# New start addresses for the stationary sides of TensorE's in, state and up projections

## What is computed

```python
xz = layernorm(x) @ w_in                          # w_in 256 x 1024
xp, z = split(xz)                                 # 512 and 512
xc = silu(causal_conv(xp, 4 taps) + conv_b)
h[t] = 0.9 * h[t-1] + 0.1 * (xc[t] @ w_B)         # 16 states
x = x + ((h @ w_C) * silu(z)) @ w_out             # w_out 512 x 256
# per sequence, the two best of 8 experts by its first token:
x = x + mean over 2 experts of (gelu(layernorm(x) @ W1[e] + b1[e]) @ W2[e] + b2[e])
```

## Time and profile before

| | |
|---|---|
| median of 3 runs | 509.88 us (509.74 to 510.04) |
| the profiled execution | 509.51 us |
| its span, first to last instruction | 507.6 us |
| PE busy | 502.6 us, 99% |
| PE weight loads | 447.5 us, 88% |
| VectorE busy | 450.1 us, 89% |
| ScalarE busy | 401.2 us, 79% |
| GpSimd busy | 343.0 us, 68% |
| chain that ended last | PE 97%, VectorE 2%, DMA 1% |

### The profile page before, as it was taken

How to read it: one execution, slowest core, us unless ns; L and a number is a source line. 1 busy time by engine, 2 the same in 40 slices (tenths; PEclk the granted TensorE clock), 3 DMA queues, 4 the chain that set the end, 5 groups by cost and what they waited for, 6 DMA issues and landing times.

```text
span 507.6 us, 9831 instructions
## 1 busy us (share of the span) xinstructions
PE 502.6 (99%) x3026; PEld 447.5 (88%) x3026; DVE 450.1 (89%) x898; ACT 401.2 (79%) x694; POOL 343.0 (68%) x386
## 2 busy tenths in 40 slices
PE   8999999999999999999999999999999999999997
PEld 8888799899998989989899998989989899898997
DVE  6999999989998899979999899997999889896773
ACT  4986958878969788697887969879797887969454
POOL 4956587659693696928969197772977549673391
PEclk9999999999999999999999999999999999999999
DMA  8940105335251542606234170432604333130102
GB/s 260 297 174 1 42 1 167 124 126 167 71 188 35 165 124 83 206 14 196 79 124 165 42 224 24 165 124 86 203 36 149 104 125 125 50 116 0 43 2 83
DMA packets 53378, 57.27 MB, mean 113 GB/s; under 512 B 8682, under 2 KB 49642, under 8 KB 53226
## 3 DMA queue, kind: packets, MB, share of 16 engines
q1 hardware_dynamic: 51498, 56.67, 34.3%
q10 hardware_dynamic: 1856, 0.31, 0.3%
HBM read 35.46 MB, written 21.50 MB: 112 GB/s over the span
## 4 chain that ended last, share of the span: by engine, by line
PE 97%; DVE 2%; DMA 1%; issue 0%; DVEq 0%
PE blk L1267 16%; PE blk L1268 16%; PE blk L1272 16%; PE tok L1384 12%; PE tok L1386 12%; PE tok L1385 12%; PE turn L1425 3%; PE turn L1428 3%; PE blk L1447 3%; PE turn L1219 1%; PE tok L1267 1%; PE tok L1268 1%; PE tok L1272 1%; DMA x_mid<-in_L_attn_x 1%; DVE stats_t L893 0%; DVE normed L910 0%
## 5 line engine op out<-in xcount | busy, mean ns | idle before, releaser
L968 DVE SCALAR_TENSOR_TENSOR conv<-blk,tap_w,conv 128x512 f32<-128x512 f32 x192 | 130.0, 741 | 9.1 <-ACT conv L659 8.4
L470 POOL TENSOR_TENSOR y_lo<-gate,y_hi 128x512 fp32r<-128x512 f32 x57 | 72.1, 1297 | 36.1 <-ACT y_hi L588 36.1
L1267 PE MATMUL blk<-xn_hi,w_in_hi 128*128 128x512 f32 x228 | 89.4, 392 | 0.0
L1268 PE MATMUL blk<-xn_hi,w_in_lo 128*128 128x512 f32 x228 | 89.0, 391 | 0.0
L435 POOL TENSOR_TENSOR xc_lo<-conv,xc_hi 128x512 fp32r<-128x512 f32 x59 | 70.5, 1211 | 9.1 <-ACT xc_hi L588 9.0
L1384 PE MATMUL tok<-w_out_hi,y_hi 128*128 128x256 f32 x256 | 72.1, 282 | 0.0
L1386 PE MATMUL tok<-w_out_hi,y_lo 128*128 128x256 f32 x256 | 71.9, 281 | 0.0
L1385 PE MATMUL tok<-w_out_lo,y_hi 128*128 128x256 f32 x256 | 71.9, 281 | 0.0
L1272 PE MATMUL blk<-xn_lo,w_in_hi 128*128 128x512 f32 x228 | 70.3, 389 | 0.0
L1384 PE MATMUL tok<-w_hi,hid_hi 128*128 128x256 f32 x248 | 70.0, 282 | 0.0
L659 ACT ACTIVATE conv<-blk,tap_b,tap_w 128x512 f32<-128x512 f32 x64 | 49.0, 777 | 26.2 <-PE blk L1272 23.7
(11 more groups left out here) (187 smaller groups left out, 1316.9 us busy)
## 6 DMA issues: line engine op xcount, KB each, us to landing
spill<-normed SPq DMA_DIRECT2D x25, 512.0 KB, 2.8
normed<-spill SPq DMA_DIRECT2D x100, 128.0 KB, 2.8
out<-x_mid SPq DMA_DIRECT2D x30, 256.0 KB, 2.7
x_mid<-in_L_attn_x SPq DMA_DIRECT2D x29, 256.0 KB, 2.7
x_in<-in_L_attn_x SPq DMA_DIRECT2D x14, 512.0 KB, 4.4
w_all<-in_L_ffn_W SPq DMA_DIRECT2D x2, 2048.0 KB, 11.5
b_all<-in_L_ffn_b SPq DMA_DIRECT2D x1, 1024.0 KB, 13.3
gate<-in_L_attn_w_in SPq DMA_DIRECT2D x2, 256.0 KB, 4.4
```

Source lines behind the costliest of these rows:

```text
L470: nc.gpsimd.tensor_tensor(y_lo[:, j, :], gate_of(o, j), y_hi[:, j, :].bitcast(F32), ALU.subtract).then_inc(y_lo_set, 1)
L968: nc.vector.scalar_tensor_tensor(cols, blk[j][:], tap_w[:, j, t:t + 1], cols, ALU.mult, ALU.add).then_inc(tap_added, 1)
L1267: mm(dst, whi(k), his(k), start=(k == 0), stop=False)
L1268: mm(dst, wlo(k), his(k), start=False, stop=False)
```

## The change

Two declarations become longer by 16 numbers (64 bytes) in each row, and the buffer of 64 bytes moves ahead of them. The views that the rest of the program uses have the same shapes as before.

```diff
+STEP = 16
...
-        w_in_hi, w_in_lo = sb("w_in_hi", [P, KD, 2 * DI], F32R), sb("w_in_lo", [P, KD, 2 * DI], F32R)
-        w1_hi, w1_lo = sb("w1_hi", [P, TOP_K, KD * D], F32R), sb("w1_lo", [P, TOP_K, KD * D], F32R)
+        behind_columns = sb("behind_columns", [P, STEP])
+        w_in_hi, w_in_lo = [sb(f"w_in_{part}", [P, KD, 2 * DI + STEP], F32R)[:, :, 0:2 * DI] for part in ("hi", "lo")]
+        w1_hi, w1_lo = [sb(f"w1_{part}", [P, TOP_K, KD * D + STEP], F32R)[:, :, 0:KD * D] for part in ("hi", "lo")]
         b_mix = sb("b_mix", [P, JD, P], F32R)
         c_mix = sb("c_mix", [P, DI], F32R)
-        behind_columns = sb("behind_columns", [P, 16])
```

## The result

The changed kernel takes 512.32 us in the median of 5 runs (512.11 to 512.55), the kernel before 509.92 us beside it (509.74 to 510.19): a ratio of 1.0047, with a 95% interval of 1.0036 to 1.0058. It is 2.4 us slower, where 2.1 us faster was forecast. The profiled execution took 512.32 us too.

A forecast was written before the change was run, and what follows sets the result against it. PE's start-to-start matmul distances were taken as the bound. 509.51 - 1.5 (new offsets) - 0.6 (run openings) = 507.4 us profiled; the median stands 0.37 us above, so 507.8 us, range 503.5 to 515.0.

The forecast's parts named there:

- What bounds the kernel: Whole program: PE's matmul row is busy 99% of the span, so start-to-start distances make the time; copies cost nothing.
- wrong at the root: Sign of failure: PE has new waits, or 512-column matmuls keep 226.6 ns while the time moves.
- The price of a new offset: 512-column matmuls whose loads get new offsets: gain of 1.2 ns each, 1270 x 1.2 ns = 1.5 us.
- The bound from below: 512-column matmuls: 226.6 ns is twice 113.3 ns, the best 256-column rhythm, so the gain may be 0.
- The bound for a loss: 512-column matmuls out of step with their loads cost 231.7 ns, 5.1 ns more.
- The openings: First matmuls of 512-column runs behind 256-column ones, some 42 in the program: half of 1.2 us saved, 0.6 us.
- The rival that the rhythm never settles: xp, z and up of every step: differing loads disturb each matmul, up to 5.1 ns each, 516.5 us; chance 0.35.
- The rival of the token matmuls' better rhythm: 256-column matmuls go from 117.7 to 113.3 ns, 6.4 us less, 503.5 us; chance 0.10.
- Offsets don't matter: All matmuls: new addresses change nothing since the read ports are independent, 509.9 us; chance 0.15.
- What would show it: Up projection with `state_in`: 7.21 us or less means gain, 7.25 no effect, 7.30 and above rhythm lost.
- the slower case: 512-column matmuls lose their steady rhythm, up to 516.5 us, chance 0.35; touched loads of 192 instead of 188 ns would support it.

The follow-up runs named there:

- the small matmuls: Kernel before plus one matmul of 8 or 64 columns (second kernel: 32 or 128) ahead of looped 256-column runs: 508.53 and 508.85 us.

## Why the prediction was wrong

- *What bounds the kernel.* Right: PE's distances alone, with no cost at the copies. The one new wait of PE, 0.5 us in the opening, would have been a sign of being wrong at the root by the prediction's own words, but the first projection starts no later with it.
- *The price of a new offset.* This is the step that failed: "I take half of the gain, 1.2 ns per matmul". The sign was wrong. The price came from 256 columns, 2.3 ns cheaper at 64 than at 0, with the reason that a load is as long beside a long matmul as beside a short one. The runs show that the relation turns round with the width: at 512 columns 64 costs 6.6 ns more than 0 (516.1 us with all at 64). That loads are equally long at both widths was true (188 ns) and said nothing of what a matmul costs. The bound from below had it nearly right: 226.6 is twice 113.3, and no offset tried gave less than 226.7, so there was nothing to gain. The bound for a loss, 5.1 ns from an opening, was close to what the new offsets cost, though for another reason, since there it is an opening and here a lasting price: w_in, w1, b_mix and c_mix lost 5.48 us over 1332 matmuls, 4.1 ns each.
- *The openings.* The 0.6 us saved didn't come. The first six matmuls of z take 1394 ns now and took 1388 before, and behind them the run doesn't come back to 226.7: it repeats a pattern of six distances (229, 237, 229, 234, 228, 229, ...) at 231 ns.
- *The rival that the rhythm never settles* happened, 4.1 ns of its 5.1. It would give 509.51 + 5.5 = 515.0 us alone. (Its upper end for the profiled execution is 509.51 + 6.8 = 516.3 us, not 516.5.) Its reason was only half right: it blamed loads that differ from one another, but loads all alike at 64 are worse (516.1), and the variation helps as far as it brings in cheap offsets. Only for w1's second expert did it cost something of its own.
- *The rival of the token matmuls' better rhythm* happened as well, for the 36 of `down` and the 12 behind `state_out` in the looped steps, 2.45 us. The prediction gave it a chance of 0.10 and no part in the sum; without it the change would have cost some 4.9 us. The argument against it, that the usual run starts behind a steady run of 512 columns, holds for the kernel before but doesn't tell the cases apart: behind b_mix at a steady 233.3 ns (all at 64) `down` stays at 117.8, behind b_mix at a nearly steady 232.8 in the changed kernel it goes at 113.4. And that a run's rhythm is set as it starts is contradicted by the prediction's own, where it changes within the run.
- *Offsets don't matter.* Refuted: two kernels with the same instructions differ by 6.2 us (516.1 against 509.9). The Trainium skill (TensorE: Matmul & The Clock Gate, What happens when you issue a matmul) says that the two read ports are independent. What the prediction drew from it, that no offset can count, the measurement decides against; the page itself speaks of read bandwidth and not of start addresses.
- *What would show it.* 7.45 us for the up projection with `state_in` was read rightly as the rhythm lost. "192 would speak for the slower case" was wrong: with all at 64 z's loads last 188 ns at 233.3 ns a matmul, as they did at 227.8. In the changed kernel 36 of w1's 288 loads between 108 and 469 us last 192 ns, where none did before.

What stays open: why offset 0 is the cheapest for 512 columns and not for 256, and why two offsets 256 bytes apart cost nearly the same. That what stands ahead of a run can decide between 113.3 and 117.7 ns is shown by the small matmuls; which entries lead to which rhythm isn't. The moving sides stood at one place in every kernel, so it isn't shown whether the stationary side's own start counts or its distance from the moving side's.

## What to carry to other kernels

Where back-to-back matmuls bound a kernel, measure the distance from start to start for each kind of matmul, and vary the start address of the stationary side: a price for an offset holds for the width at which it was measured, and may turn round at another. Before a steady rhythm is given up, see whether it is the best that the kernel's rows show for that shape. And look at what stands ahead of a long run: a few slightly dearer matmuls, or one tiny one, can put the next 36 or 47 into a better rhythm, and a change can win there what it loses at its own place.

## What the runs showed of the hardware

- With the moving side at one place, a matmul's cost depends on the stationary side's start: 226.7 to 234.0 ns at 512 columns, 113.3 to 120.2 at 256. At 512 columns two starts 256 bytes apart cost the same within 1 ns.
- At 256 columns and offset 64 there are two steady rhythms at the same addresses, 113.3 and 117.7 ns. Behind one matmul of 8 to 128 columns the looped runs were always in the better one; a load 35 ns late ahead of a run, or distances of 121 to 125 ns in the middle of one, went with a change to the better one too.
- A matmul of 8 columns costs 27 ns itself and 85 ns more in the next one, and saves some 4 ns in each of the 47 behind.
- At 256 columns and offsets 0 and 64 the share of loads that last 192 instead of 188 ns goes with the rhythm (nearly all at 120.0, every third at 117.7, hardly any at 113.3). At 512 columns it doesn't, nor at 256 columns and offset 384 (120.2 ns with loads of 188 to 190).
